# A two-layer decoder on one core: the experts run on tokens sorted by their pair of experts

## The reference, cut to what matters

```python
scores = sigmoid(xf @ gate_w.T + lb_bias)
topw, topi = top_k(scores, 2)
topw = topw / (topw.sum(-1, keepdims=True) + 1e-08)
for e in range(8):
    m = topi == e
    wmean = (topw * m).sum() / max(m.sum(), 1)      # one weight per expert, over all 8192 tokens
    y = mlp(xf, expert_gate_w[e], expert_up_w[e], expert_down_w[e])   # silu(x g) * (x u), then down
    out = out + where(m.any(-1)[:, None], y * wmean, 0)
out = out + mlp(xf, shared_gate_w, shared_up_w, shared_down_w)
x = x + out
```

## Time and profile before

| | us |
|---|---|
| three runs, median | 3868.16 (3866.94 to 3869.19) |
| the profiled execution | 3875.04 |
| its span, first to last instruction | 3873.3 |
| granted TensorE clock, mean | 0.957 |
| PE busy | 3482.9 (90%) |
| DVE busy | 2936.8 (76%) |
| ACT busy | 2362.7 (61%) |
| POOL busy | 1369.9 (35%) |

### The profile page before, as it was taken

How to read it: one execution, slowest core, us unless ns; L and a number is a source line. 1 busy time by engine, 2 the same in 40 slices (tenths; PEclk the granted TensorE clock), 3 DMA queues, 4 the chain that set the end, 5 groups by cost and what they waited for, 6 DMA issues and landing times. The chain is left out here.

```text
span 3873.3 us, 99774 instructions
## 1 busy us (share of the span) xinstructions
PE 3482.9 (90%) x28590; PEld 2988.2 (77%) x28590; DVE 2936.8 (76%) x9302; ACT 2362.7 (61%) x8540; POOL 1369.9 (35%) x4940
## 2 busy tenths in 40 slices
PE   2779999999999999999958888888888699999999
PEld 2758888888888888888747777777777488888888
DVE  4368888888888888888737777777777666666666
ACT  1347777777777777777637777777777433333332
POOL 0034445445444454454414555555555200000000
PEclk8579999999999999999969999999999799999999
DMA  4000100000000000000010000000000100000000
GB/s 147 10 21 31 32 24 32 27 30 32 24 32 32 24 32 27 30 32 24 21 31 18 16 16 16 16 16 16 16 16 16 41 14 11 11 12 11 11 11 13
DMA packets 76035, 96.53 MB, mean 25 GB/s; under 512 B 12593, under 2 KB 65345, under 8 KB 75969
## 3 DMA queue, kind: packets, MB, share of 16 engines
q1 hardware_dynamic: 69696, 86.52, 7.0%
q0 software_dynamic: 2176, 8.39, 0.6%
q10 hardware_dynamic: 4096, 0.83, 0.1%
HBM read 78.67 MB, written 17.04 MB: 25 GB/s over the span
## 5 line engine op out<-in xcount | busy, mean ns | idle before, releaser
L365 POOL TENSOR_TENSOR tiny<-tiny 128x1 f32<-128x1 f32 x3456 | 776.7, 225 | 866.6 <-DVE tiny L352 626.2
L712 ACT ACTIVATE work<-bank,att 128x128 f32<-128x128 f32 x2048 | 722.2, 378 | 86.0 <-DVE att L702 80.5
L173 PE MATMUL bank<-w1r,workr 128*128 128x256 f32 (+2 forms) x1536 | 557.6, 363 | 12.4 <-DVE workr L1775 11.3
L175 PE MATMUL bank<-w1r,workr 128*128 128x256 f32 (+2 forms) x1536 | 514.1, 335 | 0.0
L174 PE MATMUL bank<-w1r,workr 128*128 128x256 f32 (+2 forms) x1536 | 513.8, 334 | 0.0
L702 DVE TENSOR_REDUCE att<-bank 128x4 f32<-128x512 f32 x512 | 335.0, 686 | 150.8 <-PE bank L695 143.4
L712 ACT ACTIVATION_READ_ACCUMULATOR work<-bank,att 128x1 f32 x2048 | 446.7, 218 | 0.0
L193 PE MATMUL bank<-work,w0p 128*128 128x128 f32 x3072 | 428.7, 280 | 3.2 <-ACT r_tfi_ L1078 1.8
L2136 ACT ACTIVATE work<-bank 128x256 f32<-128x256 f32 x320 | 123.6, 386 | 489.5 <-PE bank L175 489.5
L193 PEld LDWEIGHTS bank<-work,w0p 128*128 128x128 f32 x3072 | 384.2, 194 | 12.2 <-ACT work L1003 2.5
L731 PE MATMUL bank<-const,work 128*128 128x128 f32 x2048 | 317.5, 278 | 52.3 <-ACT work L737 35.2
(11 more groups left out here) (254 smaller groups left out, 8079.7 us busy)
## 6 DMA issues: line engine op xcount, KB each, us to landing
work<-decay_sums SPq DMA_DIRECT2D x64, 512.0 KB, 3.6
work<-in_ctx SPq DMA_DIRECT2D x128, 128.0 KB, 2.0
x_res<-in_x POOLq DMA_DIRECT2D x8, 1024.0 KB, 19.8
recurrence_out<-r_xo_ SPq DMA_DIRECT2D x64, 128.0 KB, 1.7
work<-recurrence_out SPq DMA_DIRECT2D x64, 128.0 KB, 2.1
out_dram<-work SPq DMA_DIRECT2D x64, 128.0 KB, 1.7
work<-in_L_attn_in_proj_w SPq DMA_DIRECT2D x10, 128.0 KB, 13.1
work<-in_L_ffn_expert_gate_w SPq DMA_DIRECT2D x8, 128.0 KB, 2.2
```

Of the source, the lines that this page charges most:

```text
L173: pe.matmul(out_, lhs[0], rhs[0], start=first, stop=False)
L175: return pe.matmul(out_, lhs[1], rhs[0], start=False, stop=last)
L365: e.tensor_tensor(out_, a_, b_, ALU.add if b_ is three_halves else ALU.mult)\
L712: last = e.activation(Pb[g % 2][:, c * P:c * P + P], sc_banks[g % 2][:, c * P:c * P + P], ACT.Exp, bias=a_nm[:, 4 * g + c:4 * g + c + 1], ...
```

## The change

Two experts out of eight give 28 unordered pairs. The tokens are sorted by their pair, each pair's tokens filling whole tiles of 128 rows; at most (8192 + 28 x 127) / 128 = 91 such tiles are needed, and always 91 are run.

- Before `layer1`'s loop, POOL fills a scratch tensor in DRAM (`pair_rows`, 92 x 128 rows of 516 floats) with blank rows whose token number lies outside the output.
- `route` numbers each token's pair, counts tokens per pair and tile with 28 one-column matmuls, forms ranks and starting places with triangular matmuls, and makes an owner table (two expert columns per sorted tile) on partition 0. The weight pieces are loaded in two parts (12, then 26).
- `experts` has two loops. The first (64 tiles) runs only the shared MLP and scatters, per token, the normalised row, residual plus shared result, two weights, the token's number and its place, as one row of 2064 bytes, from POOL. The second (91 tiles) loads a sorted tile (SP), loads the two owners' columns into PE's registers, runs one pair of experts with weights addressed by those registers, adds, and scatters the 1 KB rows to the output by token number (POOL). Rows outside the output are skipped. Both loops have a body of eight tiles and a ring of eight row buffers.

```diff
+                e.memset(blank, 0.0).then_inc(S["blank_ready"], 1)
+                e.iota(blank[:, 0, 2 * D + 2:2 * D + 3].bitcast(I32), [[0, 1]], base=TOKENS, channel_multiplier=1)
+                for k in range(4):
+                    e.dma_start(slots.rearrange("(s k p) d -> k p s d", k=4, p=P)[k],
+                                blank.to_broadcast([P, BLANKS // 4, ROW])).then_inc(S["blank"], 16)
...
+                for q in range(PAIRS):                                    # route, PE
+                    last = e.matmul(bank[7][0:NB, SPARE + q:SPARE + q + 1], t_hot[:, :, q], const[:, C_ONE:C_ONE + 1],
+                                    start=True, stop=True)
+                last.then_inc(S["t_tiles"], 1)
+                e.wait_ge(S["t_prefix"], 1)
+                for g in range(4):
+                    e.matmul(bank[4 + g][:, 0:SPARE], r_up, t_hot[:, 16 * g:16 * g + 16, :], start=True, stop=False)
+                    e.matmul(bank[4 + g][:, 0:SPARE], const[0:NB, C_ONE:C_ONE + P], t_prod[0:NB, 16 * g:16 * g + 16, :],
+                             start=False, stop=True)
...
+                e.tensor_tensor(t_hot, t_id.unsqueeze(2).to_broadcast([P, NB, PAIRS]),        # route, DVE
+                                r_pair.unsqueeze(1).to_broadcast([P, NB, PAIRS]), ALU.is_equal).then_inc(S["t_hot"], 1)
+                w2[3](e)
...
+                link(e.tensor_tensor(t_prod, t_prod, t_hot, ALU.mult))
+                link(e.tensor_reduce(t_place, t_prod, AX.X, ALU.add))
...
+                def load(i, r, turn):                                     # experts, SP
+                    if used(i, RK):
+                        e.wait_ge(S[f"k_put{r}"], 16 * turn)
+                    e.dma_start(k_row[:, r, :], src).then_inc(S[f"k_row{r}"], 16)
...
+                shared: stage(1, transpose); stage(2, up); stage(3, turned); stage(4, down)     # PE, tile i - 1, i - 2, ...
+                e.wait_ge(S["f_x6"], NB)
+                def columns(h, k):                                        # at k = 0 and 4 of the 8 tiles of a body
+                    got = nc.values_load_multi_w_load_instructions(
+                        owner[0:1, ds(2 * a, n)], engines=[mybir.EngineType.PE], min_val=0, max_val=(E - 1) * D, ...)[1]
+                def k_up(i, r, turn):
+                    e.wait_ge(S["k_lo"], i + 1)
+                    if used(i, 2): e.wait_ge(S["k_h"], i - 1)
+                    for x_ in range(2):
+                        of = ds(column[r, x_], 2 * P)
+                        for k in range(2):
+                            last = mm3(e, bank[q][:, 2 * P * x_:2 * P * x_ + 2 * P], (f_T[q][:, 0, k, :], f_T[q][:, 1, k, :]),
+                                       (w_gu[:, 0, k, of], w_gu[:, 1, k, of]), k == 0, k == 1)
+                slot: stage(3, k_transpose); stage(4, k_up); stage(5, k_turned); stage(6, k_down)
...
+                shared: stage(1, low); stage(0, norm); stage(5, finish); stage(2, gated); stage(3, hidden)   # DVE
+                slot: stage(7, k_result); stage(3, k_low); stage(4, k_gated); stage(5, k_hidden)
...
+                def norm(i, r, turn):
+                    if used(i, RF):
+                        e.wait_ge(S[f"f_put{r}"], 16 * turn)
...
+                def scatter(i, r, turn):                                  # experts, POOL, stage 5
+                    e.wait_ge(S["f_x6"], i + 1)
+                    e.indirect_dma_start(slots, bass.IndirectOffsetOnAxis(f_row[:, r, 2 * D + 3:ROW].bitcast(I32), 0),
+                                         f_row[:, r, :], None, bounds_check=last_slot).then_inc(S[f"f_put{r}"], 16)
+                def spread(i, r, turn):                                   # stage 7
+                    e.wait_ge(S["k_y"], i + 1)
+                    e.indirect_dma_start(tokens_out,
+                                         bass.IndirectOffsetOnAxis(k_row[:, r, 2 * D + 2:2 * D + 3].bitcast(I32), 0),
+                                         k_y_[:, r, :], None, bounds_check=last_token, oob_is_err=False).then_inc(S[f"k_put{r}"], 16)
```

More of the change, by code:

```diff
@@ L73, in constant_table @@
     t[:, C_3_2] = 1.5
+    t[:, R_UP:R_UP + P] = np.triu(np.ones((P, P)), 1)
+    t[:, R_SLOT] = np.arange(P)
+    t[:, R_PAIR:R_PAIR + PAIRS] = np.arange(PAIRS)
+    pairs = np.array([(E - 1 - j, E - 1 - i) for j in range(E) for i in range(j)])
+    t[:, R_STEP:R_STEP + 2 * (PAIRS - 1)] = (D * np.diff(pairs, axis=0)).T.reshape(-1)
+    t[:, R_TOK:R_TOK + TOKENS // P] = np.arange(P)[:, None] + P * np.arange(TOKENS // P)[None, :]
     return t
@@ L1970, in _ @@
                 w2[2](e)
+                w3[2](e)
             @block.vector
@@ L2032, in decoder @@
[L2032 to L2050, removed]
+        k_y_ = wk(8 * D).rearrange("p (r d) -> p r d", r=8)
@@ new lines, in decoder, with rounds, one, stage @@
+        w_dn2 = w_dn.rearrange("p s j d -> p s (j d)")
+        tokens_out = out.rearrange("b t d -> (b t) d")
+        assert wpos[0] <= WORK - 4 * NB
+        def rounds(e, n, ring, lag, step, ahead=None):
+            first = -(-(lag + ring) // ring) * ring
+            def one(h, k):
+                def stage(back, do):
+                    r = (k - back) % ring
+                    turn = h + (k - back - r) // ring
+                    i = ring * turn + r
+                    if not isinstance(h, int) or 0 <= i < n:
+                        do(i, r, turn)
+                if ahead and k % 4 == 0:
+                    ahead(h, k)
+                step(stage)
+            for i in range(first):
+                one(i // ring, i % ring)
+            with e.Fori(first // ring, n // ring) as h:
+                for k in range(ring):
+                    one(h, k)
+            for i in range(n // ring * ring, n + lag):
+                one(i // ring, i % ring)
@@ L2054, in _ @@
             def _(e):
[L2055 to L2063, removed]
+                for r in range(RF):
+                    e.wait_ge(S[f"f_put{r}"], 16 * (NB // RF))
@@ L2116, in tail, with shared @@
-                def tail(h):
-                    n, b, g, q, k = later(h, -1)
-                    turn(n, q)
-                    down(*later(h, -2))
-                    down(*later(h, -1))
-                transpose(0, 0)
-                pairs(e, steps, tail)
+                def shared(stage):
+                    stage(1, transpose)
+                    stage(2, up)
+                    stage(3, turned)
+                    stage(4, down)
+                rounds(e, NB, RF, LF, shared)
+                e.wait_ge(S["f_x6"], NB)
@@ L2217, in tail, with shared, k_low @@
-                def tail(h):
-                    hidden(2 * NG * h - 1, 1)
-                    finish(2 * h - 1, 1, h - 1)
-                norm(0, 0)
-                low(0, 0)
-                pairs(e, steps, tail)
+                def shared(stage):
+                    stage(1, low)
+                    stage(0, norm)
+                    stage(5, finish)
+                    stage(2, gated)
+                    stage(3, hidden)
+                rounds(e, NB, RF, LF, shared)
+                def k_low(i, r, turn):
+                    q = r % 2
+                    e.wait_ge(S["k_hi"], i + 1)
+                    e.tensor_tensor(f_T[q][:, 1], bank[6 + q][:, 0:D].rearrange("p (k t) -> p k t", k=2),
+                                    f_T[q][:, 0].bitcast(F32), ALU.subtract).then_inc(S["k_lo"], 1)
```

441 lines of the change are left out of this document (302 added, 139 removed).

## The result

The changed kernel takes 3585.49 us (median of 4 runs, 3583.79 to 3589.74), the kernel before 3868.68 (4 runs, 3866.94 to 3870.48): a ratio of 0.927, with a 95% interval of 0.9254 to 0.9286, so 283 us less. Forecast were 3598 and 270 less. One execution of a later kernel, x11_place, took 4000.55 us at a mean granted clock of 0.73 and is left out of its median.

What follows compares the result with a forecast made beforehand. The prediction took PE's matmuls in the experts stage to bound the kernel. Experts -303, route +28 and layer 1 +5 made -270 us from the median 3868.16, giving 3598 us, with a range of 3545 to 3715.

Steps and rivals of the forecast that it cites:

- What bounds the stage: Experts stage: PE's matmuls in a row are the bound; array work per tile 2.55 us in first loop, 2.57 in second.
- First loop, 179 us: Experts, 64 shared-MLP tiles at 2.7 us each, plus 6 us to fill and drain.
- The sign of 2.6 to 2.8 us a tile: First loop: if the forecast is right, gate activations come every 2.6 to 2.8 us.
- Change of loops, 8 us: Between the expert loops: last scatter, first sorted load and first transposes put 8 us on the path.
- Second loop, 264 us and 7 to fill: Experts, 91 sorted tiles at 2.9 us, above the array's 2.57 for register loads, plus 7 us filling at low clock.
- Loop edges, 3 us: Expert loops: 15 edges between bodies of eight tiles cost 3 us, at most 18.
- End, 4 us: End of the second loop: 4 us for the last scatter.
- Route, +28: Route stage: 64.7 us against 37.2, +28 us all on the path, bounds 20 and 45.
- Layer 1, +5: Head of layer 1: blanking issue by POOL adds 5 us, its writes hidden; bounds 0 and 45.
- Array-bound throughout: Rival for both expert loops: tiles at 2.55 and 2.57 us, edges and fills hidden, experts 422, whole 3555 us; chance 0.2.
- The sequencer as the second loop's bound: Rival: PE's register loads and address sums make a sorted tile 3.9 us, whole 3690 us; chance 0.28.
- Slower by the scatters: Rival in both expert loops: POOL's scatters take up to 19.8 us to land, whole 4070 us; chance 0.07.

Runs made afterwards that it cites:

- x11_place: Changed kernel with blanking in the steps stage, bf16 prefix products, no final POOL drain, and second-loop register loads placed behind the transposes; median 3563.1 us.
- x1_fixed: Changed kernel with the second loop always running experts 0 and 1 at constant addresses, without register loads or address sums; median 3577.6 us.
- x9_nodrain: Changed kernel with POOL's drain at the end of the experts stage left out; median 3582.3 us, experts stage 433.4 us.

## Why the prediction was right, and where its terms were not

**What bounds the stage.** Right: the array, before and after, but for 0.16 us of each sorted tile. The sum of a tile from the distances between starts gave 2.55 and 2.57; measured are 2.546, and 2.58 without register loads.

**First loop, 179 us.** Measured 170 to the last shared product (3142.3 to 3312.3). The forecast's 2.7 a tile took DVE for nearly as long as PE, with part of its register arithmetic exposed. DVE is the busier for it (145.93 of 177) but never the bound. The sign of 2.6 to 2.8 us a tile was missed on the fast side. -9.

**Change of loops, 8 us.** 7.0 by the trace.

**Second loop, 264 us and 7 to fill.** Measured 252.3, from 3319.3 to DVE's drain at 3571.6. The tile is 2.74 and not 2.9; the cause named, registers in PE's in-order queue, is right, its size was half. A load of 12 registers takes 0.85 us, far below the forecast's bound of 12 x 0.33. The shortest of the row above, of two registers, takes 0.55, the first, of four, 0.78, and the longest, of ten, 1.09: the time does not go by the count. -19.

The Trainium skill (Runtime: NRT & Kernel Launch, Instruction fetch mechanics) gives about 200 ns a register, even in bulk, when speaking of loads from HBM. This load, of 12 registers from an SBUF tile, took 71 ns a register, so the trace disagrees by nearly three; the load of two took 273. Its other rule, a fetch stall at a far branch, shows in no trace: x1_fixed runs its turns at 8 x 2.58 with the branch in them. Whether the branch's target lay outside the fetched window, no view here tells, so the rule is not refuted.

**Loop edges, 3 us.** None beyond that: -3. The 0.9 us behind the branch is in the 2.74.

**End, 4 us.** Measured 11.0. The forecast priced the landing of the last scatter, 4 us, and that was right (SP passes at 3575.3, 3.7 us behind DVE's drain); it put nothing for the drain of POOL, which takes 9.4 us and ends 7 later: +7. x9_nodrain gives 7.0 of it back. The experts together: 465 - 9 - 1 - 19 - 3 + 7 = 440.

**Route, +28.** Measured +37.6, inside its bounds of 20 to 45, and the largest miss upwards. The step that failed: "the 256-wide start every (1.03 - 0.39)/3 = 0.21 us, so 0.37 each at full clock and 0.74 at half: 5". Rows 12 calls its x4 four products; they are two products of two instructions each, so a product of 448 columns costs twice that in columns, 1.49 at half clock, and 0.3 more with its loads: 1.79 us, eight of them 14.3. The stage's clock was 0.54, before and after, so even by the forecast's own price half clock and 5.9 were due, and not 5. The one-column products were put at 3 and took 6.6, for the same reason. The rest of the stage came out 3 us below its sum.

The Trainium skill (Perfetto Trace Analysis, Engine Utilization) halves the array's rate for a low-high fp32 product. By that alone, as an estimate, 448 columns at the 1.2 GHz level would be 0.75 us. A single instruction here fits it (0.9 us with its load), but the trace has two of them for one product.

**Layer 1, +5.** Measured +6.8. The size is near by luck: POOL's issue took 6.0 us for 10 and made the first Newton steps 2 us late for 5, and the writes, which the forecast had "beside loads that are asked for a tile (16 us) ahead and land in 2, so hidden", held DVE up for 7.6 us at a load that was asked for 2 us ahead. The 1.6 to 3.5 us by which layer 1 without blanking is shorter than before's hide the rest.

**The rivals.** Array-bound throughout: that is the first loop, and the second with x1_fixed; its 422 for the experts is nearer to the measured 440 than the forecast's 465. The sequencer as the second loop's bound at 3.9 a tile: no, the array idles 0.16 of 2.74. But its sign, PE idle with "issue" as the releaser, did show, at a small price. Slower by the scatters: no, POOL waits for DVE, the last landing takes about 2 us, and the ring bore two scatters for one. Its sign showed too, SP's loads waiting for a DMA (104.3 us), and meant nothing, since PE waited for a loaded row only once.

**The total.** By terms, experts -25, route +10, layer 1 +2 against the forecast: 13 us faster than it, which is what the medians say (3585 for 3598). That the total is so near is in part luck: 32 us too much in the two loops stand against 19 too little in the end, the route stage and layer 1. The two profiled executions lie 290 us apart and the medians 283; layer 0, whose clock went one way before and the other after, was 8.9 us shorter in the profiled one of after, which is of that size. Whether it is the cause can't be told, as the other executions left no trace.

## What to carry to other kernels

Price an fp32 product from a row whose instruction count you have checked against the code: one product was two instructions, and exact small integers could go in bf16 for about a quarter of the time with 448 columns and half of it with one. When PE reads addresses from registers, count the loads, and look at what PE's queue holds at that moment; the rest of the addressing was nearly free. Add up the end of the program too, up to the last drain. And when a bulk write runs beside small loads, look at how far ahead those loads are asked for while the pipeline fills, and not only in its steady part.

## What the runs showed of the hardware that was not expected

POOL's drain at the end of a stage with indirect DMAs took 8.1 to 11.5 us in the runs, and 8.07 when every DMA had already landed; in layer 1, whose POOL had issued only plain DMAs, all landed, it took 0.5. In the first stage, where POOL issues the loads of x, it took 34.7 us, until 0.8 us after the last of their packets; there other engines ended later. A load of 128 KB that landed in 2 us otherwise took over 9 beside blanking writes at 297 GB/s. An empty scatter, all of whose rows are out of bounds, still took POOL 0.98 us and moved 576 bytes. A second load whose values nobody used was dropped by the compiler, so a doubled cost has to be looked for in the trace before its time is believed. And the same code of layer 0 ran in one of two ways, 1783 to 1787 or 1789 to 1795 us, with a granted clock of 0.99 or of 0.89 to 0.93 between 250 and 365 us.
